# Experts on sorted tiles of 128 rows: each token scattered to its two experts, the shared expert in two halves around them

## What is computed

```python
x = hidden_states.reshape(-1, h)                      # 4096 tokens x 256
scores = softmax(x @ gate_w, axis=-1)                 # 8 experts
topk_w, topk_idx = top_k(scores, 2)
topk_w = topk_w / (sum(topk_w) + 1e-20)
for e in range(8):                                    # w_gate, w_up: 256 x 512, w_down: 512 x 256
    hid = silu(x @ w_gate[e]) * (x @ w_up[e])
    y = y + w_per_expert[:, e:e + 1] * (hid @ w_down[e])
shared = silu(x @ ws_gate) * (x @ ws_up) @ ws_down
out = layernorm(x + y + shared)
```

## Time and profile before

| what | us |
|---|---|
| three executions | 4113.43, 4109.88, 4111.06 (median 4111.06) |
| the profiled execution's own time | 4093.74 |
| its span, first to last instruction | 4092.0 |
| first attention, from its fills to the next block | 193 to 1077 |
| router, from its first transfer | 2837.5 to 2876.2 |
| expert matmuls | 2876.2 to about 4083 |

### The profile page before, as it was taken

One profiled execution on the slowest core, in us unless ns is written; L12 is line 12 of the kernel. 1 busy time (PEld: TensorE's weight loads), 2 busy tenths in 40 slices (PEclk: granted clock), 3 DMA queues, 4 the chain that ended last, 5 costly groups with the idle time before them and its releaser, 6 DMA issues. The chain is left out here.

```text
span 4092.0 us, 57437 instructions
## 1 busy us (share of the span) xinstructions
PE 3600.8 (88%) x17708; PEld 2420.9 (59%) x17708; DVE 2255.1 (55%) x3301; ACT 1487.2 (36%) x2424; POOL 1072.6 (26%) x819
## 2 busy tenths in 40 slices
PE   8889999999799968799966588855899999999999
PEld 6644454545244426444435466643788888888888
DVE  5577777777366645566646455556433333333345
ACT  3236666666443433233333143332222222222222
POOL 4510000000043334333334500011333333333332
PEclk9979999999799988799987698877999999999999
...
GB/s 245 279 68 64 64 63 63 63 63 37 80 81 85 83 73 217 152 83 83 83 108 134 132 87 88 86 93 63 16 16 15 0 15 15 15 5 10 0 5 36
DMA packets 218074, 303.72 MB, mean 74 GB/s; under 512 B 27679, under 2 KB 133511, under 8 KB 217927
## 3 DMA queue, kind: packets, MB, share of 16 engines
...
q10 hardware_dynamic: 4224, 4.19, 0.4%
...
## 5 line engine op out<-in xcount | busy, mean ns | idle before, releaser
L564 DVE TENSOR_REDUCE an_m<-an_psm 128x1 f32<-128x1024 f32 x512 | 604.9, 1220 | 193.4 <-PE an_psm L488 191.8
L544 ACT ACTIVATE an_probs<-an_pst 128x512 f32<-128x512 f32 x1024 | 533.4, 602 | 258.4 <-PE an_pst L515 258.0
L2360 POOL TENSOR_TENSOR ex_hb<-ex_hid,ex_ha 128x512 fp32r<-128x512 f32 x288 | 377.1, 1309 | 771.9 <-DVE ex_ha L2441 771.9
L2411 ACT ACTIVATE ex_gated<-ex_pg 128x512 f32<-128x512 f32 x288 | 172.8, 600 | 925.6 <-PE ex_pg L47 925.6
L2439 DVE TENSOR_TENSOR ex_hid<-ex_gated,ex_pu 128x512 f32<-128x512 f32 x288 | 198.1, 688 | 479.7 <-PE ex_pu L47 477.2
L488 PE MATMUL an_psm<-an_ks,an_qs 95*128 95x512 f32 x1024 | 369.4, 445 | 33.1 <-DMA an_vs<-scr_v 29.6
L515 PE MATMUL an_pst<-an_qs,an_ks 96*128 96x512 f32 x1024 | 340.0, 410 | 10.1 <-issue 5.9
L488 PEld LDWEIGHTS an_psm<-an_ks,an_qs 95*128 95x128 f32 x1024 | 181.3, 199 | 269.7 <-issue 206.9
L2394 PE MATMUL ex_py<-ew_a,ex_hb 128*128 128x256 f32 x1152 | 321.7, 279 | 0.0
L2394 PE MATMUL ex_py<-ew_b,ex_ha 128*128 128x256 f32 x1152 | 321.6, 279 | 0.0
L2394 PE MATMUL ex_py<-ew_a,ex_ha 128*128 128x256 f32 x1152 | 321.4, 279 | 0.0
...
...
## 6 DMA issues: line engine op xcount, KB each, us to landing
...
ca_qs<-scr_cq SPq DMA_DIRECT2D x24, 512.0 KB, 8.4
ca_ks<-scr_ck SPq DMA_DIRECT2D x24, 512.0 KB, 10.1
mc_qs<-scr_mq SPq DMA_DIRECT2D x24, 512.0 KB, 8.5
mc_ks<-scr_mk SPq DMA_DIRECT2D x24, 512.0 KB, 10.3
scr_q<-in_ab SPq DMA_DIRECT2D x16, 512.0 KB, 2.8
```

Of the source, the lines that this page charges most:

```text
L544: act.activation(probs[:, s % 2, j], pst[:, (GH * s + j) % RING], ACT.Exp, scale=HD ** -0.5).then_inc(exp_done, 1)
L564: dve.tensor_reduce(m1[:, hq, col:col + 1], psm[:, n % 2], AX.XY, ALU.max).then_inc(mx_done, 1)
L2360: pool.tensor_tensor(hb[:, f], hid[:, f % 2], ha[:, f].bitcast(F32), ALU.subtract).then_inc(b_done, 1)
L2411: act.activation(gated[:, f % 2], pg[:, f % 2], ACT.Silu).then_inc(gated_done, 1)
```

## The change

Experts work on sorted rows. `route` also counts, for each expert, the tokens before each token (two matmuls with a triangle and a square of ones, then prefix sums on VectorE), and derives for each token its two row numbers (`x_slot`) in a buffer where each expert's rows start at a multiple of 128, for each tile of 128 rows its expert (`x_which`), and for each expert the count of tiles at which its weights are free (`x_until`). The buffer has NTILE = 71 tiles, the most that 8192 pairs can need. In `run_experts`:

1. The shared expert runs on the first 8 of 16 blocks of 256 tokens. Meanwhile GpSimd scatters the rows of `x_acc` by 64 indirect transfers of 128 rows to `scr_xs` in DRAM, then loads the first four tiles.
2. Each of 71 tiles: TensorE turns the 128 rows (2 transposes), makes gate and up with the turned rows as stationary operand and the weights as moving one (12 matmuls of 512 columns), turns hidden (4 transposes), and makes the output (12 matmuls of 256 columns). ScalarE stores the rows to `scr_ys` and loads the tile six ahead. TensorE reads the tile's expert from `x_which` into a register, since the weights' address depends on it.
3. The shared expert runs on the other 8 blocks. Meanwhile GpSimd gathers, by 64 indirect transfers of 128 rows, the two rows of each token into a ring of four tiles (`ex_got`); VectorE adds them with their weights (`combine`), a pair of tiles at a time, and ScalarE normalises.

The split weights come ready from DRAM (`scr_ws`, both parts): GpSimd loads, splits and stores them in 27 pieces during the first attention, where it also blanks `scr_xs`. There the filled rows now reach from 64 to 127 and the maximum stands in row 127. One clearing of the semaphores is added after `join_attention`.

```diff
-        ONE, LAST = 4 * HD, 6 * HD
+        ONE, LAST = 4 * HD, P
...
+G0, U0, D0 = 0, KH * D, 2 * KH * D
+EW = D0 + FB * H
+SLOTS = P
+NTILE = 2 * TOK // SLOTS + NE - 1
+XROWS = (NTILE + 1) * SLOTS
+BT = 2
+SHARED = TOK // (BT * P)
...
+                e, m = pieces[n]
+                src = expert_matrices(A, e)[m].rearrange("(k p) n -> p k n", p=P)
+                pool.dma_start(wraw[:, n % 2].rearrange("p (k n) -> p k n", n=src.shape[-1]), src).then_inc(raw_in[n % 2], 16)
...
+            blank = scr["xs"].rearrange("(i p r) h -> i p (r h)", p=P, r=PIECE // H)
+            for i in range(XROWS * H // (P * PIECE)):
+                pool.dma_start(blank[i], zeros[:]).then_inc(zero_out, 16)
+            for n, (e, m) in enumerate(pieces):
+                pool.wait_ge(raw_in[n % 2], 16 * (n // 2 + 1))
...
+                pool.wait_ge(hi_done, n + 1)
+                pool.tensor_tensor(wpair[:, n % 2, 1], wraw[:, n % 2], wpair[:, n % 2, 0].bitcast(F32), ALU.subtract)\
+                    .then_inc(lo_done, 1)
+                pool.wait_ge(lo_done, n + 1)
+                pool.dma_start(scr["ws"][e * P:(e + 1) * P, :, m * PIECE:(m + 1) * PIECE], wpair[:, n % 2].bitcast(F32))\
+                    .then_inc(pair_out[n % 2], 16)
+                if n + 2 < len(pieces):
+                    load_piece(n + 2)
+            pool.wait_ge(zero_out, 16 * (XROWS * H // (P * PIECE)))
...
+            for e, n in ((NE, 0), (0, 1)):
+                sp.dma_start(w[:, n], scr["ws"][e * P:(e + 1) * P]).then_inc(experts_in, 16)
+            sp.wait_ge(experts_in, 32)
...
-            pool.tensor_tensor(expert_b[:, 0], expert_raw[:, 0], expert_a[:, 0].bitcast(F32), ALU.subtract)\
-                .then_inc(expert_b_done, 1)
-            pool.wait_ge(expert_b_done, 1)
...
+            pe.matmul(counted[:, 0], upperF[:], both[:], start=True, stop=True)
+            pe.matmul(counted[:, 1], onesF[:], both[:], start=True, stop=True).then_inc(c_ready, 1)
...
+            link(dve.tensor_tensor(place[:], running[:], within[:], ALU.subtract))
+            link(dve.tensor_tensor(place[:], place[:], shift[:].unsqueeze(2).broadcast_to([P, NE, TT]), ALU.add))
+            link(dve.tensor_tensor(place[:], place[:], counted[:, 0], ALU.add))
+            for n, onehot in enumerate((first, second)):
+                link(dve.tensor_tensor(onehot[:], onehot[:], place[:].rearrange("p e t -> p t e"), ALU.mult))
+                link(dve.tensor_reduce(where[:, n], onehot[:], AX.X, ALU.add))
...
+            link(dve.tensor_scalar(which[:], expert[:], float(NE - 1), None, ALU.min))
+            link(dve.tensor_scalar(until[:], end[:], float(BT * SH1), None, ALU.add))
...
+        NX = 4
+        FIRST = 2 * SH1
+        SECOND = FIRST + NTILE
+        LAST = NTILE - 1
+        ROUNDS = (NTILE - 3) // 4
+        REST = range(4 * ROUNDS + 1, NTILE)
...
+            sp.wait_ge(y_ready, BT * SH1)
+            load(1, 0)
+            sp.wait_ge(w_in, 16)
+            sp.sem_inc(w_ready, 1)
+            for e in range(2, NE + 1):
+                freed = sp.value_load(until[0:1, e - 2:e - 1], min_val=1, max_val=BT * SH1 + NTILE)
+                sp.wait_ge(y_ready, freed)
+                load(e, (e + 1) % 2)
+                sp.wait_ge(w_in, 16 * e)
+                sp.sem_inc(w_ready, 1)
...
+                if tt >= NGB:
+                    pool.wait_ge(scattered[tt % NGB], 32 * (tt // NGB))
                 for n in range(2):
-                    expert(2 * ep + n, n, True)
-            expert(NE, 0, False)
+                    pool.indirect_dma_start(scr["xs"], bass.IndirectOffsetOnAxis(ap=slot[:, n, tt:tt + 1], axis=0),
+                                            acc[:, tt], None).then_inc(scattered[tt % NGB], 16)
+            for n in range(NGB):
...
+            pool.sem_inc(rows_gone, 1)
+            for i in range(NX):
+                pool.dma_start(xrow[:, i], x_v[i]).then_inc(first_rows, 16)
+            pool.wait_ge(first_rows, 16 * NX)
...
+            for n in range(2):
+                pool.wait_ge(y_out[n], 16 + 16 * ((NTILE + 1 - n) // 2))
+            for tt in range(TT):
+                if tt >= NGB:
+                    pool.wait_ge(two_done, tt - NGB + 1)
+                for n in range(2):
+                    pool.indirect_dma_start(got[:, tt % NGB, n], None, scr["ys"],
+                                            bass.IndirectOffsetOnAxis(ap=slot[:, n, tt:tt + 1], axis=0)).then_inc(gathered[tt % NGB], 16)
...
+            def turn(i, buf, uses):
+                pe.wait_ge(x_in[buf], 16 * uses + 16)
+                if not (isinstance(i, int) and i == 0):
+                    pe.wait_ge(xb_done, i)
+                for kh in range(KH):
+                    last = pe.transpose(psx[:, kh, 0:SLOTS], xrow[:, buf, kh * P:(kh + 1) * P], ident[:])
+                last.then_inc(xT_ps, 1)
...
+            def turn_hidden(i, par):
+                pe.wait_ge(hid_done, FIRST + i + 3)
+                for f in range(FB):
+                    last = pe.transpose(psh[:, f], hid[:, par, f * P:(f + 1) * P], ident[:])
...
+            def expert_of(i):
+                return pe.value_load(which[0:1, bass.ds(i, 1)], min_val=0, max_val=NE - 1)
+            def hidden(i, par, e, at):
+                pe.wait_ge(w_ready, e + 2)
+                pe.wait_ge(xb_done, i + 1)
+                for dst, first, free, ready in ((pg, G0, gated_done, g_ready), (pu, U0, hid_done, u_ready)):
+                    pe.wait_ge(free, FIRST + i + 1)
+                    last = mm3(pe, dst[:, par], [xsa[:, par, n] for n in range(KH)], [xsb[:, par, n] for n in range(KH)],
+                               [matrix(at, 0, first, n, D) for n in range(KH)], [matrix(at, 1, first, n, D) for n in range(KH)])
+                    last.then_inc(ready, 1)
...
+            def down(i, par, at):
+                pe.wait_ge(b_done, FIRST + i + 1)
+                pe.wait_ge(y_taken, i + 1)
+                for f in range(FB):
+                    da, db = (matrix(at, part, D0, f, H) for part in range(2))
+                    for n, (x, y) in enumerate(((ha, da), (ha, db), (hb, da))):
+                        last = pe.matmul(py[:, par, 0:H], x[:, par, f * P:(f + 1) * P], y, start=(f == 0 and n == 0),
+                                         stop=(f == FB - 1 and n == 2))
+                last.then_inc(y_ready, 1)
...
+                    turn(0, 0, 0)
+                if c:
+                    pe.wait_ge(acc_done, BT * c)
+                shared_down(2 * c, 0)
+            turn(1, 1, 0)
+            pe.wait_ge(acc_done, BT * SH1)
...
+            with pe.Fori(0, ROUNDS) as r:
+                es = [expert_of(4 * r + n) for n in range(5)]
+                ats = [offset(e) for e in es]
+                for n in range(1, 5):
+                    hidden(4 * r + n, n % 2, es[n], ats[n])
+                    down(4 * r + n - 1, (n - 1) % 2, ats[n - 1])
+                    turn(4 * r + n + 2, (n + 2) % NX, r + (n + 2) // NX)
+                    turn_hidden(4 * r + n, n % 2)
...
+            for c in range(SH2):
+                u = SECOND + 2 * c
+                if c:
+                    shared_hidden(SH1 + c, u, WS)
+                    pe.wait_ge(acc_done, BT * (SH1 + c))
+                else:
+                    shared_hidden(SH1, u, WS, lambda: down(LAST, LAST % 2, ats[-1]))
+                    pe.wait_ge(y_taken, NTILE + 2)
+                shared_down(u, WS)
...
+            def load(i, buf):
+                act.dma_start(xrow[:, buf], x_v[bass.ds(i, 1)].rearrange("o p h -> p (o h)")).then_inc(x_in[buf], 16)
...
+            def keep(i, par, uses):
+                act.wait_ge(y_ready, FIRST + i + 1)
+                act.wait_ge(y_out[par], 16 * uses + 16)
+                act.activation(yrow[:, par], py[:, par, 0:H], ACT.Copy).then_inc(y_taken, 1)
+                act.wait_ge(y_taken, i + 3)
+                act.dma_start(y_v[bass.ds(i, 1)].rearrange("o p h -> p (o h)"), yrow[:, par]).then_inc(y_out[par], 16)
...
+            def deviations(q):
+                act.wait_ge(mv_done, BT * q + BT)
+                act.activation(std[:, q % 2], mv[:, q % 2, :, 1], ACT.Sqrt, bias=eps[:]).then_inc(std_done, 1)
...
+            def combine(q):
+                for n in range(BT):
+                    tt = BT * q + n
+                    dve.wait_ge(acc_done, tt + 1)
+                    dve.wait_ge(gathered[tt % NGB], 32 * (tt // NGB) + 32)
+                    dve.scalar_tensor_tensor(out=acc[:, tt], in0=got[:, tt % NGB, 0], scalar=share[:, 0, tt:tt + 1], in1=acc[:, tt],
+                                             op0=ALU.mult, op1=ALU.add).then_inc(one_done, 1)
+                for n in range(BT):
+                    tt = BT * q + n
+                    dve.wait_ge(one_done, tt + 1)
...
+                    dve.wait_ge(norm_done, BT * (q - 1))
+                for n in range(BT):
+                    dve.wait_ge(stats_done, BT * q + n + 1)
```

(16 more changed lines are left out.)

474 lines of the change are left out of this document (299 added, 175 removed).

## The result

| | executions | us, median (range) |
|---|---|---|
| before | 4 | 4112.06 (4109.88 to 4113.43) |
| changed | 4 | 3647.22 (3642.56 to 3650.97) |

The account below looks back on a forecast made before the run. TensorE's matmuls were taken to bound the kernel, busy for 88% of the span. 2885 + 94 + 396 + 120 gave 3495 us of span, 3497 as execution, 3514 with 17.3 added; 8-in-10 range 3415 to 3700.

Parts of the forecast that it names:

- experts begin: Start of expert work: 2876.2 before, plus 7 for first-attention cover and clearing, plus 2 for the router: 2885.
- first half: Shared expert's first 8 blocks beside 64 scatters, until tile 0 can start: 94 us, bounds 67 and 203.
- tiles: Loop over 71 tiles: 354 us at 4.99 each plus 42 of idle at 17 round heads, 396 us.
- second half and end: Shared expert's last 8 blocks beside the gathers, then the remaining pairs: 70 + 45 + 5 = 120 us.
- What goes: Expert matmuls: 103 units of 128 rows in place of 288, taking 431 us in place of 1206.
- allowance of 17.3: Added to the profiled execution's forecast of 3497 because the earlier median lay 17.3 above its profiled execution: 3514.
- 67 are covered: First half: of 94 us of scatters and loads, 67 run under TensorE's matmuls and 27 are its wait.
- T: Time of one indirect GpSimd transfer in both shared-expert halves: taken as 1.3 us, bounds 0.375 and 2.9.
- rival on GpSimd's transfers: Shared expert's halves: VectorE and GpSimd shut each other out, transfers take 2.0 us: 3588, at 2.9 3706; chance 0.17.
- just too short for this: Tile loop: the 2.5 us idle gap per round was taken as too short to lower TensorE's clock.
- third rival: Tile loop: gaps reach 3 us, about 8 us behind each run at 1.2 GHz: 3642; chance 0.08.
- end behind TensorE: After TensorE's last matmul: 45 us for nine pairs left, 5 for the last scaling and store.

Follow-up runs that it names:

- e8: Kernel before with only the new first attention, GpSimd's weight and blank pieces in it, and the semaphore clearing; old router and experts: 4103.3 us, ratio 1.0006.
- e6: Changed kernel with only the high-part product, a third of the matmuls, in the shared expert's first half: 3564.9 us, one run.
- e5: Changed kernel with 2 shared-expert blocks before the tiles and 14 behind, in place of 8 and 8: 3582.4 us, ratio 0.8749.
- e10: Changed kernel with register loads spread in the tile loop and 2 shared-expert blocks before the tiles, 14 behind: 3517.4 us, ratio 0.8569.
- e3: Changed kernel with the 64 scatters as plain GpSimd transfers of the same rows, left unsorted: 3548.5 us, one run.
- e2: Changed kernel with one register load left at each tile round's head, the others behind gate and up matmuls: 3538.8 us, ratio 0.8637.
- e7: Changed kernel with GpSimd clearing an unused 128x1536 area, about 1.3 us, after each of the 64 scatters: 3636.2 us, one run.

## Why the prediction was right, and where it was short

The sum was 3495 us of span; the trace has 3648.3. By its own terms:

| term | forecast | trace | off |
|---|---|---|---|
| experts begin | 2885 | 2908.5 | +23.5 |
| first half | 94 | 154.4 | +60.4 |
| tiles | 396 | 447.4 | +51.4 |
| second half and end | 120 | 138.0 | +18.0 |

That is 153.3. The median lies 2.8 below the profiled execution, and I had added 17.3, so 133 remain.

- **What goes: right.** 103 units in place of 288. Undisturbed shared blocks take 9.20 us, not 8.37, and tiles inside a round 4.87, where 4.99 was forecast.
- **Before the experts: right.** e8 bounds the side work at 0 to 7 us. Router start to first expert matmul is 38.6 us, as long as before. The allowance of 17.3 was in effect the spread upstream: the profiled execution of before was an early one, that of after a late one. That it offsets most of the 23.5 is luck.
- **First half: the step that failed is "67 are covered".** T was 1.28 against 1.3 and the landings as forecast; e6 and e5, where tile 0 waits for the scatters alone, take 94.4 and 95.4 (e10, with the stop, 96.3). But I priced the scatters as a list of their own, beside which TensorE runs on. It didn't: the scatters took 84 us with their landing, 70 us more passed behind them, in which most of the blocks ran, and e3 with 77 in all shows that the indirect form does it. The rival on GpSimd's transfers had a slower GpSimd; the trace has a GpSimd at its forecast speed and everything else stopped. On that rival's page of the Trainium skill (SBUF — State Buffer, SBUF: two separate sides): the scatters were spaced at 1.28 us whether VectorE cast beside them or not (in e6 the median of 20 spacings beside a cast is 1.28, that of the 44 others 1.27). By that page's rule, under which such a cast keeps GpSimd from writing its lists, GpSimd would have been the one held; the trace does not agree. The range held all the same, but partly by luck: it reached up to 3700 for this rival, whose cause did not show, and that room took in the 60 and 51 us of the two misses.
- **Tiles: the size of the gap, and the step "just too short for this".** A load with its register work comes every 0.80 us (0.7 forecast), 306 ns of it the load itself. The branch adds 0.5, so the gap is 3.55 us in place of 2.5: 17 x 1.05 = 18. Behind it the clock fell, as the third rival had it, at 25.4 - 4 x 4.87 - 3.55 = 2.4 us a round: 41. Less 71 x 0.12 = 9 for the faster tiles, 50 of the 51.4. e2 took out both at once, for 1.05 us a round that stayed. I had the two rows that show this clock behind a gap of 3.06 us and gave it 0.08. The Trainium skill (DMA: Bandwidth & Descriptors, Latency and other measured facts) names about 600 ns as the least for such a load; measured were 306, and the measurement decides.
- **Second half and end.** The end behind TensorE was right: 52.6 us for 50, with GpSimd's 1.27 us per gather as its pace (line L2480: 0.95 us each in the median and 0.3 between). TensorE's part took 85.4 in place of 70: 7 for the blocks' 9.20, the rest for the stops beside the gathers, which e6 and e7 did not have.
